# Four-layer gated cross-attention with experts: reading attention scores from PSUM on VectorE, and layer norms on ScalarE

## What is computed

```python
x = x + tanh(g_xattn[1]) * xattn1(layernorm(x), ctx, ctx, key_bias, Wq, Wk, Wv, Wo)
x = x + tanh(g_ffn[1])   * ffn1(layernorm(x), ...)
# xattn1: 16 heads of 16
scores = einsum('bhqd,bhkd->bhqk', q, k) / sqrt(16) + key_bias[:, None, None, :]
out = einsum('bhqk,bhkd->bhqd', softmax(scores), v) @ Wo.T
```

## Time and profile before

| | us |
|---|---|
| median of 3 runs | 1342.4 (1341.94 to 1349.6) |
| profiled execution, its own time | 1342.16 |
| its span, first to last instruction | 1340.5 |
| loop of layer 1 in the trace, first to last low part | 427.3 to 571.6 |
| loop of layer 3 in the trace, first to last low part | 1091.8 to 1216.7 |

### The profile page before, as it was taken

How to read it: one execution, slowest core, us unless ns; L and a number is a source line. 1 busy time by engine, 2 the same in 40 slices (tenths; PEclk the granted TensorE clock), 3 DMA queues, 4 the chain that set the end, 5 groups by cost and what they waited for, 6 DMA issues and landing times. The chain is left out here.

```text
span 1340.5 us, 26537 instructions
## 1 busy us (share of the span) xinstructions
PE 1036.2 (77%) x8492; PEld 771.8 (58%) x8493; DVE 800.2 (60%) x1767; ACT 554.9 (41%) x1319; POOL 578.3 (43%) x738
## 2 busy tenths in 40 slices
PE   5778287886558999940999916799987879997998
PEld 3666167784335777730899802455555557776443
DVE  4576163443383789865555544346663648886876
ACT  2452023342124666634343315556651257773000
POOL 1473703555344777634000062546662257772000
PEclk9986588998678999855999956889998979996999
DMA  3463208883113111147777421000001000000000
GB/s 110 117 178 122 102 3 289 293 296 119 54 32 114 48 36 36 48 168 283 250 254 253 168 70 53 1 1 1 1 1 47 2 12 17 16 18 6 16 23 24
DMA packets 70682, 123.47 MB, mean 92 GB/s; under 512 B 15481, under 2 KB 41859, under 8 KB 70595
## 3 DMA queue, kind: packets, MB, share of 16 engines
q1 hardware_dynamic: 63011, 101.64, 22.8%
q0 software_dynamic: 7584, 20.72, 4.6%
HBM read 52.98 MB, written 24.64 MB: 58 GB/s over the span
## 5 line engine op out<-in xcount | busy, mean ns | idle before, releaser
L2472 PE MATMUL bank<-l0f_x_high,l_weights 128*128 128x256 bf16 x256 | 51.0, 316 | 33.4 <-issue 20.2
L2881 POOL DMA_DIRECT2D l_results<-keep x23 | 12.5, 544 | 135.6 <-DVE keep L2984 129.7
L303 ACT ACTIVATE xnT<-bank 128x256 f32<-128x256 f32 (+1 forms) x112 | 41.3, 380 | 70.1 <-PE bank L292 69.3
L3256 PE MATMUL bank<-l_weights,room 128*128 x552 | 65.1, 273 | 4.3 <-DVE room L3284 2.9
L3244 PE MATMUL bank<-room,xnT 128*128 128x128 bf16 x1104 | 67.6, 223 | 0.0
L3244 PEld LDWEIGHTS bank<-room,xnT 128*128 128x128 bf16 x1104 | 65.8, 100 | 0.3
L2304 DVE SCALAR_TENSOR_TENSOR l3f_total<-bank,l3f_share,l3f_total 128x256 f32<-128x256 f32 x112 | 54.2, 484 | 15.6 <-PE bank L2222 12.0
L1849 POOL TENSOR_TENSOR l2x_probs<-l2x_probs,l2x_inverse 128x333 f32<-128x333 f32 x64 | 49.1, 789 | 29.0 <-DVE l2x_inverse L1755 29.0
L2687 PE MATMUL bank<-room,l0r_placed 128*128 128x128 bf16 x936 | 61.3, 224 | 0.0
L3256 PEld LDWEIGHTS bank<-l_weights,room 128*128 128x128 bf16 x552 | 52.7, 98 | 12.4 <-issue 5.4
L2687 PEld LDWEIGHTS bank<-room,l0r_placed 128*128 128x128 bf16 x936 | 58.2, 101 | 0.6
(11 more groups left out here) (437 smaller groups left out, 3162.5 us busy)
## 6 DMA issues: line engine op xcount, KB each, us to landing
xnT<-l_weights SPq DMA_DIRECT2D x23, 1024.0 KB, 5.1
l0r_placed<-l_weights SPq DMA_DIRECT2D x39, 512.0 KB, 3.6
l0w_staging<-in_L_ffn_weights SPq DMA_DIRECT2D x16, 480.0 KB, 3.8
l_weights<-in_L_ffn_weights SPq DMA_DIRECT2D x16, 384.0 KB, 3.1
room<-in_L_ffn_weights SPq DMA_DIRECT2D x12, 512.0 KB
room<-l_rows SPq DMA_DIRECT2D x39, 128.0 KB, 3.2
l_results<-room POOLq DMA_DIRECT2D x39, 128.0 KB, 3.1
xnT<-in_L_ffn_weights SPq DMA_DIRECT2D x8, 512.0 KB, 7.9
```

Source lines behind the costliest of these rows:

```text
L303: act.activation(self.chip.xnT[:, :, span(t, P)], bank[:, 0:DIM].rearrange("p (k n) -> p k n", k=KD), ACT.Copy).then_inc(self.copied, 1)
L2472: last = pe.matmul(self.bank[:, c, branch * width:(branch + 1) * width], self.weights[w][:, at:at + P], x[:, s, k, :], start=(i == 1), sto ...
L3256: last = pe.matmul(bank[:, 2 + u, 0:DIM], h[:, u, c * P:(c + 1) * P], expert_part(split[:, w, :, :], e, KD * hidden_width + c * DIM, DIM), ...
```

## The change

- `copy_scores`, the tile `raw` and GpSimd's `shift` go. VectorE's `maxima` works by group, straight from the score bank: a reduction over 308 elements, then a subtraction of the 4 maxima from the same bank into `probs`. The score bank is free after this subtraction, and `scores` waits for `shifted` in place of `scores_copied`.
- `exponents` is done in two halves of 616 elements; `transpose_probs` waits for its half. The factor 1/4 moves into the constant `head_of`, which GpSimd's spreading of the keys applies, and the scaling of the key bias (L806) goes.
- Scores are made one tile ahead, each group right behind the transposes of the same group. `project_q` and `copy_q` serve the next batch item and move from u = 1 to u = 0.
- The norm is applied by ScalarE: `scalar_apply` with 1/sigma as scale and a new column, minus mean over sigma, as bias. GpSimd makes the column with two more small operations per norm. `scalar_apply` stands behind the exponents and `copy_q`, ahead of `feed.high`. In layer 1 ScalarE applies both norms; VectorE keeps the share (`vector_share`).
- GpSimd's norm work for t-2 moves to the head of tile t, spreading of keys from u = 0 to u = 1.
- Gate logits of the last tiles: 8 at a time in the last tile, in place of 2 at four points of the last two.

```diff
     def power(self, pool, t, u, n=1):
+        if self.by_scalar:
+            mean = self.moments.mv[:, at, 0:1].rearrange("p n a -> p (n a)")
+            minus_one = self.constants[:, 4:5].to_broadcast([P, n])
+            pool.tensor_tensor(self.offset[:, at], mean, minus_one, ALU.mult).then_inc(self.negated, n)
         pool.wait_ge(self.shifted_done, t + n)
         pool.tensor_tensor(self.rstd[:, at], shifted, minus_half, ALU.pow).then_inc(self.rstd_ready, n)
+        if self.by_scalar:
+            pool.wait_ge(self.rstd_ready, t + n)
+            pool.wait_ge(self.negated, t + n)
+            pool.tensor_tensor(self.offset[:, at], self.offset[:, at], self.rstd[:, at], ALU.mult).then_inc(self.offset_ready, n)
+    def apply_by_scalar(self, act, t, u, rows, out):
+        act.wait_ge(self.offset_ready, t + 1)
+        act.activation(out, rows, ACT.Identity, scale=self.rstd[:, u:u + 1],
+                       bias=self.offset[:, u:u + 1]).then_inc(self.normed, 1)
...
 (TensorE)
+                    for g in range(GROUPS):
+                        transpose_probs(t, u, g)
+                        if u == 0:
+                            scores(b, 1, b % 2, (g,))
+                        elif ahead >= 1:
+                            scores(b + 1, 0, (b + 1) % 2, (g,))
+                        if g == 1 and not first:
+                            transpose_mixed(t - 1)
+                        if g == 2 and not first:
                             project_out(t - 1)
+                    if u == 0 and ahead >= 1:
+                        project_q(b + 1)
+                    if u == 1 and ahead == 0:
+                        chip.logits.some(pe, 8, norm)
                     attend(b, t)
                     if not is_step(b, 0):
                         norm.tensor(pe, t - 2, u)
...
 (ScalarE)
+            def exponents(t, u, half):
+                act.wait_ge(shifted, GROUPS * t + 2 * half + 2)
+                at = slice(2 * half * width, 2 * (half + 1) * width)
+                act.activation(probs[:, u, at], probs[:, u, at], ACT.Exp).then_inc(probs_ready, 1)
...
+                    high_probsT(t, 0)
+                    high_probsT(t, 1)
+                    if not is_step(t, 0):
+                        copy_mixedT(t - 1)
+                    high_probsT(t, 2)
                     if ahead >= 1 or u == 0:
+                        exponents(t + 1, 1 - u, 0)
+                    high_probsT(t, 3)
+                    if ahead >= 1 or u == 0:
+                        exponents(t + 1, 1 - u, 1)
+                    if u == 0 and ahead >= 1:
+                        copy_q(b + 1)
+                    if not is_step(b, 0):
+                        norm.scalar_apply(act, t - 2, u)
                     feed.high(act, b, u)
                     if not is_step(b, 0):
                         norm.scalar(act, t - 2, u)
...
 (VectorE)
+            def maxima(t, u, g):
+                dve.wait_ge(scores_ready, GROUPS * t + g + 1)
+                heads = slice(g * GROUP, (g + 1) * GROUP)
+                scores_of = s_bank[g % 2][:, 0:width].rearrange("p (h k) -> p h k", h=GROUP)
+                dve.tensor_reduce(row_max[:, u, heads], scores_of, AX_X, ALU.max).then_inc(max_ready, 1)
+                dve.wait_ge(max_ready, GROUPS * t + g + 1)
+                wait(dve, probs_transposed, GROUPS * (t - 1))
+                dve.tensor_tensor(probs[:, u, g * width:(g + 1) * width].rearrange("p (h k) -> p h k", h=GROUP),
+                                  scores_of, row_max[:, u, heads].unsqueeze(2).to_broadcast([P, GROUP, KEYS]),
+                                  ALU.subtract).then_inc(shifted, 1)
...
+                    for g in range(GROUPS):
+                        low_probsT(t, g)
+                        if ahead >= 1 or u == 0:
+                            maxima(t + 1, 1 - u, g)
                     if not is_step(b, 0):
-                        norm.vector_apply(dve, t - 2, u)
-                        norm.vector_apply_again(dve, t - 2, u)
+                        norm.vector_share(dve, t - 2, u)
                     if not is_step(t, 0):
                         update_x(t - 1, 1 - u)
                     normalise(t)
```

136 lines of the change are left out of this document (42 added, 94 removed).

## The result

The changed kernel takes 1380.73 us (median of 4 runs, 1376.4 to 1381.43) against 1344.34 for the kernel before, run beside it: ratio 1.0258, 95% interval 1.0219 to 1.0298. It is slower, and by 13 us or so more than the forecast's +23.1. The profiled execution has a span of 1378.5 against 1340.5.

A forecast was written before the change was run, and what follows sets the result against it. The prediction took a tile's chain of dependent steps, not a full engine, as the bound. Loops +15.3 and +12.3, starts -5.0 and -3.9, ends +1.4 and +3.0 gave +23.1 on 1342.2: 1365 us, range 1343 to 1386.

The forecast's parts named there:

- The chain: Layer loops, low part to low part: rounds, half exponential, query copy, apply, transposes, high part; layer 3 8.91 or 9.67 us.
- the sign: Whole kernel: slower, +23.1 us in sum; slower by over 1% given 0.71.
- The terms: Layer 3's tile: apply 0.58 us, reduction from PSUM 0.470, subtraction 0.475, a round of them with the low part 1.50.
- Rival 2: VectorE's rounds: both PSUM passes at their lower bounds, 18 us less over 28 tiles, no change at 1347; 17%.
- The starts: Before the loops only tile 0 is prepared: first low parts sooner by 3.9 us in layer 1, 5.0 in layer 3.
- Layer 1's loop: Two applies ahead of VectorE's share: tiles of 10.2 and 10.8 us, loop 153.3 against 141.0, +12.3.
- Layer 3's loop: First to last low part: tiles of 8.91 and 9.67 us, loop 136.8 against 121.5, +15.3.
- rival 3: TensorE's clock drops to its low level after waits for the apply; eight more such tiles give +22: 1387; 10%.
- The ends: Behind the loops, longer queues and a dearer last norm: +1.4 us in layer 3, +3.0 in layer 1.
- The two orders: Layer ends: last mixed copy behind tile 14's apply, half the gate logits ahead of the last attend; part of +1.4 and +3.0.
- The forecast's own case: Whole kernel: the longer chain makes it slower, 1365 us, from 1350 to 1380; 62%.
- Rival 1: Loops: round trip hidden, VectorE's own work is the tile, 7.9 us in layer 3, 8.4 in layer 1; 1320; 11%.

The follow-up runs named there:

- early apply: Changed kernel with ScalarE's scalar_apply(t-2) moved ahead of the second half of the exponentials: 1330.28 us, ratio 0.9899.
- PSUM half alone: Changed kernel with the norms left on VectorE, scores still reduced and subtracted straight from PSUM: 1347.8 us, ratio 1.0038.
- the apply and the queries put right: Changed kernel with scalar_apply ahead of the second half exponential, query projection and copy split over two tiles, projection behind the last scores: 1275.77 us beside 1296.14, ratio 0.9849.
- norm half alone: Kernel before, its scores, shifts and exponentials kept, with the norms applied by ScalarE: 1392.52 us, ratio 1.0366.
- the first four experiments: Early apply (1330.28 us), PSUM half alone (1347.8), norm half alone (1392.52), and the changed kernel with three unused TensorE matmuls in odd tiles (1372.3).
- the last: PSUM half alone plus one GpSimd subtraction per tile that nobody reads: 1359.51 us beside 1346.2, ratio 1.0095.

## Why the prediction was right, and where it fell short

**The chain, and the sign: right.** The first low part of a tile comes when the last subtraction, the half exponential, the query copy, the apply, the norm's transposes and the high part are through. The early apply cuts that and takes 50 us out of the changed kernel, the clock's share included, with no operation gone.

**The terms.** Three durations by source line of the kernel after (ns: min/median/max):

```profile
L247 ACT ACTIVATE l3x_xn<-x_res,l3x_ln_offset,l3x_ln_rstd x16: 583/589/599, 1127.6 to 1262.6; 128x256 f32<-128x256 f32 x10, 128x256 f32 x6
...
L1146 DVE TENSOR_REDUCE l3x_row_max<-bank x64: 464/465/479, 1092.8 to 1242.5; 128x4 f32<-128x308 f32 x64
...
L1149 DVE TENSOR_TENSOR l3x_probs<-bank,l3x_row_max x64: 477/479/480, 1093.3 to 1243.0; 128x308 f32<-128x308 f32 x64
```

Forecast were 0.58, 0.470 and 0.475; a round of 1.50 was forecast and measured. The Trainium skill's rate ("VectorE: DVE Perf Modes", "The TRN2 errata") gave 0.446 as an estimate; the trace has 0.465, and 0.479 for the subtraction. Rival 2, cheap rounds, falls with this. Its rule to copy out of PSUM first holds only in part: the PSUM half alone costs 0.4%, and with the apply early the kernel that reads PSUM twice is 1% faster than the one that copies; a kernel that copies and applies early wasn't run.

**The starts: right** (-3.8 and -4.7 for -3.9 and -5.0). The 3.8 could be luck by the table alone, since what lies ahead of layer 1 varies by 4 us between the traces of this group; but inside the stage, from the first read of a score bank to the first low part, it is 12.1 for 15.9, and 9.4 for 14.1 in layer 3. **Layer 1's loop: right but for 2.1**: 10.3 to 10.5 and 10.8 to 11.4 for 10.2 and 10.8, VectorE waiting about 2.1 (25.6 in 12 times) for the second apply where 1.6 was drawn.

**Layer 3's loop: mechanism right, a term missing.** The forecast summed its intervals to 136.8; measured 144.1. Of the 7.3 between them 6.3 go with TensorE's lower clock, by the loop at 137.8: 1.5 in the first interval, which the forecast had as 8.5 and which took 10.1, and 4.8 behind the waits for the apply. The prediction had TensorE wait "1 us or more for the apply" and gave the consequence to rival 3 with 10%, all or nothing: 22 us and a clock under 0.85 in a loop. What came is in between: the wait is 1.67 in odd tiles, the clock of the loop 0.92, the price 4.8 (the 6.3 between 144.1 and the 137.8 with the three unused matmuls, less the 1.5 of the first interval). It should have stood in the sum as a share, not beside it as a case. Its argument against itself, "layer 3 runs at 0.96 with waits of 0.75 in each tile", was true of 0.75 and said nothing of 1.67.

**The ends: mis-sized.** +4.6 and +5.0 for +3.0 and +1.4. The two orders that the term was counted from were worth nothing where they were tried, and the rest of the term stays open.

**The range held, with little room.** The forecast's own case was 1350 to 1380, and 1380.7 lies at its upper edge: near it because the misses of the loops and the ends all add to the same side, and inside the stated range because that took rival 3's price in.

**Rival 1** was dismissed for the right reason (the lists are in order), but its time of 1320 was good: with the apply and the queries put right the ratio is 0.9849, which would be 1324 beside a kernel of 1344. And what its case called VectorE's gain, 1.45 for the norm, was no work of VectorE: 1.0 of it was the wait for GpSimd's subtraction, which the other half of the change removes anyway. Moving the apply to ScalarE is worth 0.3 in the odd tiles of layer 3 (8.21 to 7.90) and nothing in the even ones (8.62), 0.7 in the odd tiles of layer 1 (9.2 to 8.5) and 0.2 in the even ones (9.0), if it stands where nobody waits for it.

## What to carry to other kernels

When work is moved to an engine with an in-order list, price its place as well as its duration: here 0.59 us of activation behind a half exponential cost 50 us, and ahead of it, where the engine was idle anyway, nothing. Halves of a change don't add: +0.4% and +3.7% alone, +2.6% together. The norm half alone pays for GpSimd's list, in which a subtraction stands behind other work; the other half removes that subtraction, and with the norm operations at the end of that list the norm half alone costs +1.7%. And once a loop is near balance, look for which engine bounds which tile: work that comes every second tile (the query projection) is best cut so that each tile carries its part, outside the stretch in which the bounding engine runs through.

## What the hardware showed that was not expected

- VectorE's apply from and to SBUF takes 0.40 alone and up to 2.48 beside a GpSimd operation; its passes from PSUM are not touched (0.48 in both).
- TensorE's clock fell behind six of the seven waits of 1.67 in layer 3's loop, and three unused matmuls in these tiles kept it at 0.99 (0.92 without): adding TensorE work made the loop 4.8 us shorter from tile 1 on.
- The kernel before took 1344 to 1346 us beside the first four experiments and the last, on two chips, and 1293 to 1296 beside the others, on three. In the traces the whole difference lies ahead of layer 1: in two kernels with the apply early, its first low part came at 424.2 on a chip of the first kind and 371.8 on one of the second, and from there to layer 3's first one it was 653.0 and 652.1. It sits in one stage of layer 0: TensorE, with nothing to wait for that the trace shows, was idle 52.6 us in 36 times before its weight loads at L2475 in the first, and 6.9 in one time in the second. ScalarE's tanh behind these matmuls waited 48 to 52 us for a releaser that is not in the trace, in all seven traces of the first kind and in none of the second. Why TensorE issues them slowly there is not shown.
